# W_out loaded later, and the SSM half-unit of a two-layer recurrent kernel put in another order

## The reference

```python
    x = L0_attn_x
    xn = _layernorm(x, axis=-1)
    s = _L0_attn_ref(xn, ...)               # linear attention, 16 heads, 4 key/value heads
    g = _silu(_L0_ffn_ref(xn, ...))         # mixture of 8 experts and a shared one
    x = x + s * g
    xn = _layernorm(x, axis=-1)
    s = _L1_attn_ref(xn, ...)               # state space mixer (SSM), 32 heads of 64
    g = _silu(_L1_ffn_ref(xn, ...))         # quantized FFN, 704 hidden
    x = x + s * g

    # _L1_attn_ref
        zxbca = x @ W_in.T
        x_t, z_t, b_t, c_t, a_log = jnp.split(zxbca, [...], axis=-1)
        decay = jnp.exp(-jnp.exp(a_log))
        def step(states, inp):
            xt, bt, ct, dec = inp
            states = states * dec[:, :, None, None] + xt[..., None] * bt[:, :, None, :]
            yt = jnp.einsum('bhpn,bhn->bhp', states, ct) + xt * D
            return (states, yt)
        ...
        y = y * jax.nn.silu(z_t)
        y = (y - mu) * jax.lax.rsqrt(var + EPS) * gamma + beta
        return y @ W_out.T
```

## Time and profile before

| | us |
|---|---|
| median of 3 runs | 1802.15 (1801.72 to 1805.13) |
| the profiled execution's own time | 1803.97 |
| its span, first to last instruction | 1802.2 |
| PE busy | 1652.1 (92%) |
| DVE busy | 1153.2 (64%) |
| ACT busy | 758.6 (42%) |
| POOL busy | 664.2 (37%) |
| 1536 projection matmuls of the SSM (line 550, w_in) | 222.3 + 203.0 + 201.9 |

### The profile page before, as it was taken

How to read it: one execution, slowest core, us unless ns; L and a number is a source line. 1 busy time by engine, 2 the same in 40 slices (tenths; PEclk the granted TensorE clock), 3 DMA queues, 4 the chain that set the end, 5 groups by cost and what they waited for, 6 DMA issues and landing times.

```text
span 1802.2 us, 29615 instructions
## 1 busy us (share of the span) xinstructions
PE 1652.1 (92%) x11068; PEld 1370.2 (76%) x11068; DVE 1153.2 (64%) x2041; ACT 758.6 (42%) x1379; POOL 664.2 (37%) x500
## 2 busy tenths in 40 slices
PE   5997899898979999999969978998989899999988
PEld 3886677796868888887938866777968788888878
DVE  4334788653857777777753347886535677777767
ACT  3333455333434444444534334553334344444445
POOL 1454444101114555444514534441012155444535
PEclk9999999999989999999979989999999999999999
DMA  2333000001224443441023320000012343343410
GB/s 76 103 103 117 18 36 1 1 1 56 71 85 127 126 133 118 129 140 49 13 70 103 108 111 19 36 1 1 1 56 71 96 139 118 122 140 126 132 33 25
DMA packets 60061, 135.68 MB, mean 75 GB/s; under 512 B 8128, under 2 KB 12736, under 8 KB 59408
## 3 DMA queue, kind: packets, MB, share of 16 engines
q1 hardware_dynamic: 59920, 133.79, 23.6%
HBM read 130.81 MB, written 2.95 MB: 74 GB/s over the span
## 4 chain that ended last, share of the span: by engine, by line
PE 65%; DVE 11%; POOL 7%; issue 6%; ACT 6%; DMA 2%; SPq 1%; POOLq 0%; DVEq 0%; ACTq 0%
PE ps L550 29%; PE ps L607 6%; PE ps L869 4%; PE ps L893 4%; PE ps L646 4%; PE ps L831 3%; POOL silu_g L450 3%; PE ps L905 3%; PE ps L586 3%; POOL rb L468 2%; POOL fw_lo L435 2%; PE ps L880 2%; PE ps L748 2%; PE ps L599 2%; PE ps L749 2%
## 5 line engine op out<-in xcount | busy, mean ns | idle before, releaser
L550 PE MATMUL ps<-xnT_hi,w_in_hi 128*128 128x512 f32 x512 | 222.3, 434 | 0.0
L550 PE MATMUL ps<-xnT_lo,w_in_hi 128*128 128x512 f32 x512 | 203.0, 396 | 0.0
L550 PE MATMUL ps<-xnT_hi,w_in_lo 128*128 128x512 f32 x512 | 201.9, 394 | 0.0
L468 POOL TENSOR_TENSOR rb<-ra,rb 128x512 f32<-128x512 f32 x80 | 117.6, 1469 | 202.9 <-DVE rb L1532 202.9
L426 POOL TENSOR_TENSOR w_in_lo<-w_raw,w_in_hi 128x1024 fp32r<-128x1024 f32 x32 | 84.2, 2631 | 272.0 <-ACT w_in_hi L951 272.0
L1653 DVE TENSOR_TENSOR_SCAN lmat<-dec,ident 128x512 f32<-128x512 f32 x128 | 165.4, 1331 | 0.0
L1342 DVE TENSOR_TENSOR hid<-ps,silu_g 128x512 f32<-128x512 f32 (+1 forms) x80 | 55.1, 689 | 163.6 <-POOL silu_g L450 106.0
L513 POOL TENSOR_TENSOR yt<-yg,sz 128x512 f32<-128x512 f32 x64 | 82.1, 1283 | 172.9 <-ACT sz L1262 165.9
L550 PE MATMUL ps<-xnT_hi,fw_hi 128*128 128x512 f32 x312 | 127.9, 410 | 17.5 <-DVE fw_lo L1360 9.8
L435 POOL TENSOR_TENSOR fw_lo<-fw_raw,fw_hi 128x512 fp32r<-128x512 f32 (+1 forms) x56 | 62.6, 1119 | 185.3 <-ACT fw_hi L981 134.7
L550 PE MATMUL ps<-xnT_hi,fw_lo 128*128 128x512 f32 x312 | 125.6, 403 | 0.0
(11 more groups left out here) (194 smaller groups left out, 4392.8 us busy)
## 6 DMA issues: line engine op xcount, KB each, us to landing
dec<-dec_dram SPq DMA_DIRECT2D x64, 512.0 KB, 4.0
w_raw<-in_w_in SPq DMA_DIRECT2D x32, 512.0 KB, 4.8
wdec<-dec_dram SPq DMA_DIRECT2D x128, 128.0 KB, 3.9
pdec<-dec_dram SPq DMA_DIRECT2D x128, 128.0 KB, 3.7
fw_raw<-in_fw SPq DMA_DIRECT2D x40, 384.0 KB, 3.2
w_raw<-in_w_qkv SPq DMA_DIRECT2D x8, 768.0 KB, 4.2
comb<-comb_dram SPq DMA_DIRECT2D x8, 512.0 KB, 3.7
w_out<-in_w_o SPq DMA_DIRECT2D x2, 2048.0 KB, 10.7
```

The lines of the kernel that those rows point to most:

```text
L468: nc.gpsimd.tensor_tensor(rb[:, k], ra[:, k], rb[:, k], ALU.add).then_inc(a_rot.sem, 1)
L550: mm = nc.tensor.matmul(out, left(l, k), right(r, k), start=(j == 0), stop=(j == len(steps) - 1))
```

## The change

Four edits. On SP, W_out of the SSM is requested in the SSM stage, after the raw weights of head 2, and no longer at the start of the second FFN. On DVE, the 32 `affine_sums` of b = 0 move from the FFN's units to SSM units 10 to 25, two in each. On PE, the order within a unit becomes: all four projections (24 matmuls), then `x_turn`, `unit_intra`, `b_turn`, `unit_from_states`, `unit_scores`, `unit_updates`. On ACT, the order follows: the copy of c and the SiLU of z come before the copies of the turned x and b, `ssm_prep` comes after those two and is now made in the unit loop for head 1 too; and the SiLU of `gate`, one instruction of 2048 columns before the loop, becomes eight of 256 columns in units 0 to 7.

```diff
@@ SyncE
-                phase_over(b, 3)
-                sp.dma_start(w_out[:], a["w_out"]).then_inc(w_out_in, 16)
...
                     weights(split_ssm(b, h), a["w_in"][h], KT * XZBC)
+                    if h == 2:
+                        sp.wait_ge(o_mm.sem, o_mm.done(b * NC + NC - 1))
+                        sp.dma_start(w_out[:], a["w_out"]).then_inc(w_out_in, 16)
@@ TensorE, ssm_unit
                     if ahead:
                         project_x(u + 1)
                         project_b(u + 1)
+                        project_c(u + 1)
+                    project_z(u)
+                    if ahead:
                         x_turn(u + 1)
                     unit_intra(u)
-                    if not ahead:
-                        project_z(u)
-                        unit_from_states(u)
-                        return
-                    project_c(u + 1)
-                    b_turn(u + 1)
+                    if ahead:
+                        b_turn(u + 1)
                     unit_from_states(u)
-                    project_z(u)
-                    unit_scores(u + 1)
-                    unit_updates(u + 1)
+                    if ahead:
+                        unit_scores(u + 1)
+                        unit_updates(u + 1)
@@ ScalarE, ssm_unit
                     b_copy(u + 1)
+                    c_copy(u + 1)
+                    z_silu(u)
                     xtok_copy(u + 1)
-                    if hf == 0 and 1 <= h and h + 1 < HP:
+                    btok_copy(u + 1)
+                    if hf == 0 and h + 1 < HP:
                         ssm_prep(h + 1, (h + 1) % 2)
-                    c_copy(u + 1)
-                    btok_copy(u + 1)
-                    z_silu(u)
+                    if u < 2 * b * HP + NC:
+                        c = u - 2 * b * HP
+                        if c == 0:
+                            act.wait_ge(f_sum.sem, f_sum.done(2 * b + 1))
+                        nc.scalar.activation(gate[:, c, :], gate[:, c, :], ACT.Silu)
...
-                ssm_prep(1, 1)
-                act.wait_ge(f_sum.sem, f_sum.done(2 * b + 1))
-                nc.scalar.activation(gate[:], gate[:], ACT.Silu)
@@ VectorE
+                    if b == 0 and 0 <= u - AFFINE_FROM < NT:
+                        affine_sums(u - AFFINE_FROM)
...
-                    if b == 0 and 3 <= u < 11:
-                        if u == 3:
-                            dve.wait_ge(w_out_in, 16 * 2)
-                        for t in range(2 * (u - 3), 2 * (u - 2)):
-                            affine_sums(t)
```

More of the change, by code:

```diff
@@ L54 @@
 SUFFIX = 8
+AFFINE_FROM = 10
 SH = 32
@@ L348, in ffn_weights @@
                 sp.dma_start(fw_raw[:, k % 2, :], src).then_inc(fw_in[k % 2], 16)
-            def phase_over(b, phase):
-                sp.wait_ge(phase_end, 4 * (b * PHASES + phase + 1))
             for j in range(NC // 2):
@@ L1712, in ssm_unit @@
                     decayed_scores(u + 1, 1)
+                    if b == 0 and 0 <= u - AFFINE_FROM < NT:
+                        affine_sums(u - AFFINE_FROM)
                 def affine_sums(t):
+                    if t == 0:
+                        dve.wait_ge(w_out_in, 16 * 2)
                     for x in range(2):
```

## The result

The changed kernel takes 1875.39 us (median of 5 runs, 1871.24 to 1879.12) against 1802.72 us for the kernel before (median of 5): a ratio of 1.0405, 95% interval 1.0381 to 1.0428. It is slower by 72.7 us, where +75 and 1877 were forecast. The profiled execution spans 1872.0 us, 69.8 more than the one before.

What follows compares the result with a forecast made beforehand. PE was taken to bound the kernel, busy 92% of the span and setting the SSM loop's pace. The terms 63.3 - 6.5 + 38 - 12.9 - 6.9 summed to +75 us on 1802.15, giving 1877 us, range 1840 less 4 to 1902.

Steps and rivals of the forecast that it cites:

- Term 2: SSM even units: the next head's weights come too late, PE waits 2.3 us; 30 x 2.11 = +63.3 us.
- Term 1: PE's order in SSM units: one projection run saves 0.29 us, junctions cost 0.1; 34 x -0.19 = -6.5 us.
- Term 3: SSM loop: PE's clock drops after 9/12 of 30 waits, 1.7 us each; +38 us, bounds 0 and +51.
- The first rival: SSM loop: the clock holds after the waits, so +37 us in all, 1840 us; chance 0.20.
- Nine of twelve: Trace of the kernel before: after nine of twelve PE waits of 2.1 to 2.9 us, the clock goes to 0.50.
- Terms 4 to 6: SSM loop's first units lose their excess, -12.9 us; affine sums leave the FFN, -6.9; W_out's load moves, 0.
- Term 5: Second FFN of b = 0 gets shorter without the affine sums, -6.9 us; in the SSM nothing, at worst +5.
- Term 6: W_out's load moved into the SSM behind head 2's raw weights: 0, or +10 us if it slows them.
- The rival of the weights in time: SSM loop: the next head's weights are ready when PE arrives, so -32 us, 1770 us; chance 0.10.

Runs made afterwards that it cites:

- e1: Changed kernel with the high part of the next head's weights made on ACT right after the copy of c: 1775.35 us, 0.9851 of the kernel before.
- e2: Changed kernel with the high part of the next head's weights made between the copies of the turned x and b: 1818.54 us.
- e7: Kernel before with only the high part of the next head's weights moved behind the copies of c and the turned b: 1818.31 us.
- e5: As e1, with PE leaving out waits that an earlier wait already covers: 1776.88 us.
- e3: Changed kernel with the old order within a unit on PE and ACT, the other edits kept: 1782.75 us.
- e6: Kernel before with only head 1's high part moved into the unit loop and the SiLU of gate in eight parts: 1789.84 us.
- e4: Kernel before with only W_out's load and the 32 affine sums moved into the SSM: 1794.48 us.

## Why the prediction was right

Term by term, against the two traces:

| term | forecast | measured in the traces |
|---|---|---|
| 2, weights late, 30 even units | +63.3 | 30 x (12.02 - 10.15) = +56 |
| 1, one run of projections, 34 units | -6.5 | -2, and -2 for the two last even units |
| 3, clock after each wait | +38 | 27 x 1.5 = +40 |
| 4, first unit | -12.9 | -12.9 |
| 5, affine sums out of the FFN | -6.9 | -4.9 here (the other element: -0.8) |
| 6, W_out's load | 0 | 0 |
| elsewhere | 0 | -4 |

**Term 2** held in its mechanism, though the profile calls the wait "issue" and not POOL's `w_in_lo`, as the forecast had it: e1 removes it, e2 takes half a microsecond of it, e7 makes it anew in the old order, each near the size counted. Its rows gave every step: from the start of the intra products, the high part at 2.18 us counted and 2.21 measured, POOL at 3.31 and 3.34. Two sizes were off: the subtraction took 2.35 us, the short end of its range (in e2 and e7 it does too; no run shows what sets it), and PE's own groups took 3.88 us from start to start in place of 3.73. So the wait is 1.85 and not 2.3 us.

**Term 1** was right in what it saves (a run of 24 projections takes 5.69 to 5.70 us) and mis-sized in what comes back: 0.1 us was taken for the new junctions, and 0.23 was measured, near the bound of 0.29. That it is not the waits, e5 shows; what in the small groups costs it stays open. The last even unit of each element gained 1.06 us (11.16 before, 10.10 after), which the forecast did not have; in e3 PE stands idle in the old order's loop for 0.94 us, and units before the last have no wait.

**Term 3** was the uncertain one, with 0, 38 and 51 as its values. Nine of twelve became 27 of 30, which came near the 38 us but does not measure the chance of one wait: the waits kept step with the falls of the clock (see e2), and the forecast had counted them as independent. The first rival, that the clock holds, was wrong for this kernel and is exactly what happens in e2, at 1818.5 us, with waits 0.5 us shorter. Its forecast of 1840 counted waits of 2.3 us.

**Terms 4 to 6** held; e6 and e4 show them alone. e4's 5 us and the 6.8 us of its FFN fit the 6.9 forecast for Term 5. The changed kernel's trace has less, since its FFN has more time at the lower clock: 0.88 in the window of 71.68 us above, against 0.91 in e1, whose code up to there is the same:

```profile
432.39:502.20 69.81, 61.33 (x307) 51.49 (x308) 37.87 (x46) 27.50 (x41) 18.24 (x10) 0.91 0.18 53
```

The raw weights right before W_out's load took 6.2 and 6.4 us to land, where the median is 4.8, in the margin that Term 6 had counted. DMA issues of the changed kernel from 527 us on:

```profile
w_out<-in_w_out SPq DMA_DIRECT2D x1, 2048.0 KB, 10.6
...
w_raw<-in_w_in SPq DMA_DIRECT2D x1, 512.0 KB, 6.2
```

The 4 us elsewhere lie between the first element's last unit and the second element's second FFN, where no edit but the last unit's order reaches. The kernel before spends more of that stretch at the lower clock, from the end of the expert FFN to the end of attention. Windows of it, before and then after:

```profile
839.26:1334.09 494.83, 440.98 (x2559) 372.19 (x2559) 291.60 (x518) 208.65 (x412) 162.90 (x132) 0.95 0.13 42
```

```profile
873.54:1363.93 490.39, 436.32 (x2562) 367.65 (x2558) 292.78 (x520) 209.29 (x412) 164.52 (x133) 0.97 0.13 44
```

The sum was closer than its terms. Against the traces it is 5 us too high: Term 2 is 7 us too high and the 4 us elsewhere were not forecast, while Terms 1, 3 and 5 together erred by some 6 us the other way. That the medians differ by 72.7 us and the two profiled executions by 69.8 is the spread of the runs, and it happened to bring the result to 2 us from the forecast. That much of it is luck; the mechanism is not.

The rival of the weights in time, 1770 us, is e1 at 1775: the mechanism and nearly the price were right, but it needed another order on ACT.

## What to carry to other kernels

When an engine is busy all the time, look first at the margin of what it will need next: here 1.24 us, with a helper instruction moved back by 3.4 (it started 5.0 us ahead of the point where PE was ready for the next head, and 1.7 us in the changed kernel). When the order on one engine is changed, go through the instructions that ride along on the others and ask for each what it must now stand behind; the copy that nothing in the unit needs, but the next unit does, belongs ahead of those that wait. A short wait that repeats can cost clock as well as idle time: here 40 us beside 56. Shortening it a little can then be worth more than what is cut off: in e2 57 us for 15 us less of waiting.

## What the runs showed of the hardware

Between waits of 1.34 us, 21.9 us apart (clock never lost in 30), and of 1.85 us, 23.9 us apart (lost in 27 of 30), each followed by dense matmuls, the difference was sharper than the twelve mixed waits of the kernel before had shown. What part of it belongs to the length and what to the distance is open.

Waits that are already satisfied cost PE nothing measurable between small matmuls: 318.27 us with and without four or five of them in each unit (e1, e5).

Small groups of matmuls cost more behind one another than between long ones, 0.23 us in a unit: the b turn 0.49 in place of 0.43 us, the products with the states 0.76 in place of 0.59. Why is open.

The affine sums, whose operands all lie in SBUF, take longer beside POOL's work on SBUF. In the changed kernel the 16 beside POOL's subtraction and sums take 0.89 to 1.50 us each, the 16 others, with POOL idle for all or half of them, 0.47 to 0.54. DVE's timeline, two in each row:

```profile
660.77 2.44 DVE L1725 SCALAR_TENSOR_TENSOR affine<-w_out,gamma_beta,affine 128x256 f32<-128x256 f32 x2
...
674.45 0.93 DVE L1725 SCALAR_TENSOR_TENSOR affine<-w_out,gamma_beta,affine 128x256 f32<-128x256 f32 x2
```

POOL's timeline of the first row's time has its subtraction until 661.50 and then a sum over y, 1.45 us long where a later one takes 1.29:

```profile
661.46 1.45 POOL L522 TENSOR_TENSOR y_sum<-y_sum,yt 128x512 f32<-128x512 f32 x1
...
665.73 1.29 POOL L522 TENSOR_TENSOR y_sum<-y_sum,yt 128x512 f32<-128x512 f32 x1
```
